# Third graph stream: weighted one-hots made on ScalarE; first experts' inner product computed transposed

## The chip, the cores and the metric

The kernel runs on one core of a Trainium2 chip. The metric is the device time of one execution in microseconds (us). The core's engines run side by side: TensorE (PE, with its weight loads shown as PEld), VectorE (DVE), ScalarE (ACT), GpSimd (POOL) and SyncE (SP), and 16 DMA engines move data. An engine executes its own instructions in the order in which they are written; engines wait for each other on semaphores.

## The reference, cut to what is computed

A graph of 6250 nodes (256 features each) and 106,250 edges sorted by target node goes through two layers. Each layer adds to `x` a graph attention of the normalised `x` and a dense mixer, then a mixture of experts. Layer 1's graph attention is itself two attention passes, so there are three edge streams: the kernel's L0, L1 and L2.

```python
xn = _layernorm(x)
x = x + _L0_gnn_ref(xn, edge_index, ...) + _L0_mix_ref(xn[None], ...)[0]
x = x + _L0_ffn_ref(_layernorm(x)[None], ...)[0]
xn = _layernorm(x)
x = x + _L1_gnn_ref(xn, ..., src, dst) + _L1_mix_ref(xn[None], ...)[0]
x = x + _L1_ffn_ref(_layernorm(x)[None], ...)[0]
# the last pass of _L1_gnn_ref (one head): the third stream
z2 = h1 @ W2.T
e2 = _leaky((z2 @ a2[:OUT_DIM])[src] + (z2 @ a2[OUT_DIM:])[dst])
alpha2 = _segment_softmax(e2, dst, n)
out = jax.ops.segment_sum(alpha2[:, None] * z2[src], dst, num_segments=n)
# _L0_ffn_ref, for each expert e of the two that a token chose
h = jax.nn.gelu(tokens @ w1[e] + b1[e], approximate=False)
y = h @ w2[e] + b2[e]
out = out + combine[:, e:e + 1] * y
```

## The kernel before

**A stream.** The edges are cut into units of 128, one edge on each partition. Two units make a slot, eight slots (16 units) a group, and there are 58 groups (`NG2`), 928 units (`NU`). For each unit GpSimd issues one indirect DMA (L1004) that gathers the 128 source rows into a ring of 48 units (three groups). `row_in` semaphores say when rows have landed; SyncE waits for the last ten units of a group and then raises `rows_there` (L981), for which VectorE waits before it adds the source scores (L1037). For each unit TensorE multiplies a 128x128 "one-hot" matrix, which says to which node of the tile each edge belongs, with the gathered rows (L1228), and VectorE adds the result of a slot into the node's sums (L1118). Every engine runs one loop over the groups; in its round `k` it computes the softmax weights of group `k`, and accumulates group `g = k - 1` in four quarters `q` of four units (`quad(g, q)` on TensorE). TensorE's and ScalarE's rounds begin when VectorE has the scores: L1037, L1039, then a transpose (L1198) and its copy `turned(k)` on ScalarE (L1292).

**Who makes the one-hots.** `Sr` holds eight of them, so two quarters. In the first two streams (L0 and L1) ScalarE's `spread(g, q)` makes four: four `Abs` of 128x128 (L1275), a wait for its own writes, and one `Relu` over all four, 128x512 (L1278); VectorE multiplies the gathered rows with the weights (L1096). In the third stream (L2, `weighted`) nothing is multiplied into the rows; VectorE makes one-hots that already carry the weight, in `weigh(g, q)`: four `tensor_scalar` of 128x128 (L1091), `is_equal` and then `mult` by a column of `WT`, the weights copied there by ScalarE's `weights(k)` (L1301). ScalarE's other work in a round is the same in all streams: two `one_hot(k + 1, v)`, each an `Abs` and a `Relu` of 128x1024 in bf16 (L1286, L1288), and `weights(k)`: `Exp` (L1298), then, after TensorE's `back(k)` (L1214, L1215), the copies (L1301 or L1303, and L1304).

**The first experts (`ffn0_*`).** Tokens are sorted into 106 tiles (`NE2`) of 128, each with one expert. GpSimd gathers a tile (L1682, ring of 12). TensorE transposes it (L1697), ScalarE copies it out (L1734, `rxe`), TensorE multiplies with the expert's first weights, picked by a register offset (L1706: the tokens are the stationary operand, the weights stream through, 256 columns), VectorE adds the bias `b1e` (L1752, `rh0`), TensorE transposes the two halves again (L1723), ScalarE applies the Gelu (L1740, `rhe`), TensorE multiplies with the second weights (L1715), VectorE adds the second bias (L1759), and SyncE writes the tile out (L1482). A product of float32 shows as two PE instructions for each `matmul` call. TensorE's loop does, in its round `r`: transposes of tile `r`, first product of tile `r - 1`, second product of `r - 3`, second transposes of `r - 2`. The routing stage ahead of it (`route0_*`) begins on TensorE when `ffn0_in` says that the router's weights, both biases and a small table have been loaded (L1475 to L1478); these four loads follow each other on SyncE's queue. The stages are separated by `meet`, where all engines wait for each other, SyncE with the last writes.

## Time and profile before

| | |
|---|---|
| median of 3 runs | 5757.75 us (5744.93 to 5762.94) |
| the profiled execution | 5751.42 us, its span 5749.6 us |
| busy over the span | PE 71%, PEld 49%, DVE 60%, ACT 48%, POOL 58% |
| third stream (3.70 to 4.94 ms) | 58 groups, about 20.7 us each |
| first experts' tiles (1.94 to 2.18 ms) | 106 tiles, about 2.17 us each |

The page of the profile gives busy shares of the whole span; the stages have different limits, so the questions below are put to views of one stage: busy time by window, instructions in order of time, and what an engine waited for. In a row of the timeline, "x4" is a merged run of four instructions with its total time, and the brackets give how long the engine had been idle before it and what ended that.

### The profile page before, as it was taken

Reading aid. Unit: us, or ns where it says so; the run is one execution under the profiler, and the core shown is the slowest. Engines: PE = TensorE matmul, PEld = TensorE weight load, DVE = VectorE, ACT = ScalarE, POOL = GpSimd, SP = SyncE. Lnnn points to the kernel's source line nnn. Section 1 sums busy time; section 2 is a strip of 40 time slices with the busy share of each in tenths; the row PEclk is TensorE's granted clock in tenths of the full one; section 3 lists DMA queues with packets and bytes.
Section 4 is the critical chain, followed back from the end, with each engine's and each line's share of the span. In section 5 each row is a group of like instructions: output and inputs, shape, how many; then the busy total and the mean of one; then the engine's idle time right before and its main releaser. Section 6 shows DMA issues by size and latency. Waiting matters only on the chain.

```text
span 5749.6 us, 74760 instructions
## 1 busy us (share of the span) xinstructions
PE 4073.4 (71%) x17795; PEld 2838.0 (49%) x17795; DVE 3468.9 (60%) x10658; ACT 2754.3 (48%) x5942; POOL 3352.1 (58%) x3492
## 2 busy tenths in 40 slices
PE   4996766666663697777777776655655656797998
PEld 3564544454443584455555555434444444333665
DVE  5377766666677537778788787745555555622111
ACT  2365666666642233578888887522222222243222
POOL 0124777777755645377777777377777777112222
PEclk9998778877875798889899898877778787898999
DMA  4293555555541333244444444344444444200110
GB/s 129 79 285 87 142 139 139 139 139 140 140 117 58 116 119 120 84 130 133 133 133 133 132 132 134 97 130 129 129 129 129 129 129 129 75 30 27 37 32 27
DMA packets 347521, 660.26 MB, mean 115 GB/s; under 512 B 78867, under 2 KB 196641, under 8 KB 346697
## 3 DMA queue, kind: packets, MB, share of 16 engines
q0 software_dynamic: 156336, 433.90, 27.8%
q1 hardware_dynamic: 180992, 213.07, 12.7%
q10 hardware_dynamic: 9772, 8.50, 0.5%
q8 instruction: 164, 2.69, 0.2%
q14 instruction: 257, 2.10, 0.1%
HBM read 541.11 MB, written 115.45 MB: 114 GB/s over the span
## 4 chain that ended last, share of the span: by engine, by line
PE 24%; issue 14%; DVE 12%; POOL 11%; DMA 5%; ACT 3%; DVEq 1%; POOLq 0%; SPq 0%; ACTq 0%
POOL AR L1004 7%; PE ps L1228 6%; DMA AR<-D_z,SRCI 4%; PE ps L2604 4%; PE ps L2585 3%; PE ps L2293 3%; POOL AR L1682 2%; PE ps L2081 2%; DVE AR L1118 1%; PE ps L2305 1%; POOL D_sx L1672 1%; PE ps L1190 1%; DVE AR L1091 1%; DVE AR L1096 1%; PE ps L2070 1%
## 5 line engine op out<-in xcount | busy, mean ns | idle before, releaser
L1004 POOL DMA_INDIRECT AR<-D_z,SRCI x1856 | 1801.3, 971 | 675.3 <-issue 496.7
L1228 PE MATMUL ps<-AR 128*128 128x264 f32 (+2 forms) x5568 | 1764.4, 471 | 212.8 <-DVE AR L1091 74.1
L1228 PEld LDWEIGHTS ps<-AR 128*128 128x128 f32 x5568 | 1240.8, 234 | 524.1 <-issue 149.9
L1004 POOL DMA_INDIRECT AR<-D_h,SRCI x904 | 872.9, 966 | 277.3 <-issue 241.6
L1118 DVE TENSOR_TENSOR AR<-ps,AR 128x264 f32 (+2 forms) x1392 | 588.2, 423 | 163.6 <-DVE AR L1118 128.2
L1275 ACT ACTIVATE AR<-iota_n,NREL 128x128 f32<-128x128 f32 x1856 | 587.3, 389 | 14.2 <-PE ps L1228 10.6
L1096 DVE TENSOR_TENSOR AR<-AR,ps 128x1024 f32<-128x1024 f32 x464 | 558.3, 1203 | 0.3 <-ACT AR L1304 0.3
L1198 PE MATMUL ps<-ident,AR 128*128 128x128 f32 (+2 forms) x174 | 61.1, 351 | 658.6 <-DVE AR L1039 658.6
L1037 DVE TENSOR_TENSOR AR<-AR 128x128 f32<-128x128 f32 (+2 forms) x174 | 49.1, 282 | 786.4 <-SPq L981 784.6
L1292 ACT ACTIVATE AR<-ps 128x128 f32<-128x128 f32 (+2 forms) x174 | 46.5, 267 | 839.1 <-PE ps L1198 834.1
L1288 ACT ACTIVATE AR<-AR,ones 128x1024 bf16<-128x1024 bf16 x348 | 399.5, 1148 | 11.3
L1286 ACT ACTIVATE AR<-AR,iota_p 128x1024 bf16<-128x1024 bf16 x348 | 394.5, 1134 | 20.3 <-DMA AR<-D_rel 20.3
L1198 PEld LDWEIGHTS ps<-ident,AR 128*128 128x128 f32 (+2 forms) x174 | 21.4, 123 | 711.8 <-issue 710.1
L1278 ACT ACTIVATE AR<-AR,ones 128x512 f32<-128x512 f32 x464 | 334.8, 722 | 15.1
L1091 DVE TENSOR_SCALAR AR<-AR,NREL 128x128 f32<-128x128 f32 x928 | 262.2, 352 | 0.0
L2516 POOL DMA_INDIRECT out<-X x57 | 56.8, 997 | 333.1 <-DVE X L2552 320.1
L1190 PE MATMUL ps<-AD,AR 128*128 x2784 | 180.3, 172 | 96.8 <-issue 46.8
L1208 PE MATMUL ps<-ones,AR 1*128 1x1 f32 (+2 forms) x696 | 73.6, 206 | 213.2 <-DVE AR L1072 212.8
L1190 PEld LDWEIGHTS ps<-AD,AR 128*128 128x128 bf16 x2784 | 135.3, 99 | 177.4 <-issue 145.8
L1298 ACT ACTIVATE AR<-AR 128x128 f32<-128x128 f32 (+2 forms) x174 | 53.8, 309 | 339.3 <-DVE AR L1082 336.5
L2585 PE MATMUL ps<-AR 128*128 x912 | 200.8, 381 | 18.3 <-ACT AR L2569 18.3
...
## 6 DMA issues: line engine op xcount, KB each, us to landing
...
AR<-D_h,SRCI POOLq DMA_INDIRECT x928
D_y<-AR SPq DMA_DIRECT2D x106, 128.0 KB, 1.7
...
```

Source lines behind the costliest of these rows:

```text
L1004: e.indirect_dma_start(out=GV[:, u % 48, :], out_offset=None, in_=D_row[L.i], in_offset=bass.IndirectOffsetOnAxis(ap=SRCI[:, u:u + 1], axi ...
L1091: t = e.tensor_scalar(Sr[:, u % 8, :], minus_n[:, :], NREL[:, u:u + 1], WT[K % 2][:, u % 16:u % 16 + 1], ALU.is_equal, ALU.mult)
L1096: e.tensor_tensor(G, G, w, ALU.mult).then_inc(m_ready, 1)
L1118: e.tensor_tensor(o, banks[n % 3][:, 0:YW], o, ALU.add).then_inc(slot_added, 1)
L1190: t = e.matmul(BK_AD[:, 3 * H * u:3 * H * u + 3 * H], OHr[v][:, 128 * (u % 8):128 * (u % 8) + 128], AD3[:, at], start=True, stop=True)
L1228: t = e.matmul(banks[n % 3][:, 0:YW], Sr[:, u % 8, :], GV[:, u % 48, L.GW - YW:L.GW], start=(i == 0), stop=(i == 1))
L1275: t = e.activation(w[:, i, :], iota_n[:, :], ACT.Abs, bias=NREL[:, u:u + 1])
L1278: e.activation(w[:, :, :], w[:, :, :], ACT.Relu, bias=ones[:, 0:1], scale=-1.0).then_inc(s_ready, 1)
L1286: e.activation(OHr[v], RBr[n % 2], ACT.Abs, bias=iota_p[:, 0:1], scale=-1.0).then_inc(*ac.up())
L1288: e.activation(OHr[v], OHr[v], ACT.Relu, bias=ones[:, 0:1], scale=-1.0).then_inc(oh_ready, 1)
L2585: t = e.matmul(ps[:, 0:256], rH2[q % 2][:, m, 128 * i:128 * i + 128], Wd[:, m, bass.ds(at, 256)], start=(m == 0), stop=(m == 7))
L2604: t = e.matmul(banks[2 + n % 4][:, 0:w], W1[:, k, 128 * m:128 * m + 128], rxt3[q % 2][:, k, 0:w], start=(k == 0), stop=(k == 1))
```

## The change

In the third stream VectorE's `weigh` makes nothing any more. ScalarE's `spread` now runs in all three streams; in the third its one `Relu` is replaced by four, one for each unit, of `weight - weight * |difference|`, with the weight as bias and its negative as scale, both read as columns (`WT` and the new `WN`, which `weights(k)` writes with one more copy). `r_ready` is waited for on ScalarE now.

In the first experts the first weights become the stationary operand: VectorE copies the expert's 128x512 block into `rw1` (ring of two, two tiles ahead), and TensorE streams the transposed tokens through its four 128x128 blocks, so the product comes out transposed. The second transposes are gone, and the Gelu reads `rh0` from SBUF in place of PSUM. The bias is loaded transposed, in two DMAs of single 4-byte elements in place of one broadcast; `ffn0_in` counts to 80 in place of 64 at all its waits.

```diff
@@ -926,7 +926,7 @@
         mark_side = AR.at
-        minus_n, WT = AR.take(128), AR.ring(2, 16)
+        WT, WN = AR.ring(2, 16), AR.ring(2, 16)
         assert AR.at <= 32156
...
         class Alone:
@@ -1087,9 +1087,6 @@
                 if L.weighted:
-                    for u in range(16 * g + 4 * q, 16 * g + 4 * q + 4):
-                        t = e.tensor_scalar(Sr[:, u % 8, :], minus_n[:, :], NREL[:, u:u + 1], WT[K % 2][:, u % 16:u % 16 + 1], ALU.is_equal, ALU.mult)
-                    t.then_inc(s_ready, 1)
                     return
...
                 w = BK_W[K % 2][:, 4 * H * q:4 * H * q + 4 * H].unsqueeze(2).to_broadcast([128, 4 * H, D])
@@ -1125,8 +1122,6 @@
             e.memset(BW[0:1, 17 * H:17 * H + 1], -BIG)
-            if L.weighted:
-                e.tensor_scalar(minus_n[:, :], iota_n[:, :], -1.0, None, ALU.mult)
             e.memset(Yv, 0.0).then_inc(y_clear, 1)
...
             at = None
@@ -1275,6 +1270,14 @@
                 e.wait_ge(*ac.now())
+                if L.weighted:
+                    p = (L.k0 + g) % 2
+                    if q == 0:
+                        e.wait_ge(r_ready, L.k0 + g + 1)
+                    for i in range(4):
+                        t = e.activation(w[:, i, :], w[:, i, :], ACT.Relu, bias=WT[p][:, 4 * q + i:4 * q + i + 1], scale=WN[p][:, 4 * q + i:4 * q + i + 1])
+                    t.then_inc(s_ready, 1)
+                    return
                 e.activation(w[:, :, :], w[:, :, :], ACT.Relu, bias=ones[:, 0:1], scale=-1.0).then_inc(s_ready, 1)
...
             def one_hot(k, v):
@@ -1299,6 +1302,7 @@
                     e.activation(WT[K % 2][:, :], w[:, 0:P], ACT.Copy)
+                    e.activation(WN[K % 2][:, :], w[:, 0:P], ACT.Copy, scale=-1.0).then_inc(*ac.up())
                 else:
...
                 e.activation(RR[:, 0:H], w[:, 128:128 + H], ACT.Exp).then_inc(r_ready, 1)
@@ -1309,24 +1313,24 @@
                     turned(k)
-                if g >= 0 and not L.weighted:
+                if g >= 0:
                     spread(g, 1)
...
                 side.after_one_hot0(e, k)
-                if g >= 0 and not L.weighted:
+                if g >= 0:
                     spread(g, 2)
...
                     one_hot(k + 1, 1)
-                if g >= 0 and not L.weighted:
+                if g >= 0:
                     spread(g, 3)
...
                 side.after_weights(e, k)
-                if k < NG2 and not L.weighted:
+                if k < NG2:
                     spread(k, 0)
...
@@ -1447,7 +1451,7 @@
         RW = AR.take(2, 8)
-        b1e, b2e = AR.take(2048), AR.take(2048)
+        b1T, b2e = AR.take(2048), AR.take(2048)
         rx = AR.ring(16, 260)
...
         smr = AR.ring(3, 5, 32)
@@ -1458,6 +1462,7 @@
         zero8 = AR.take(8)
+        rw1 = AR.ring(2, 2, 256)
         rxe, rh0, rhe = AR.ring(3, 2, 128), AR.ring(3, 256), AR.ring(3, 2, 128)
...
         AR.reset(25692)
@@ -1473,10 +1478,11 @@
             e.dma_start(RW[:, :, :], A["routerT"].rearrange("(k p) n -> p k n", p=128)).then_inc(ffn0_in, 16)
-            e.dma_start(b1e[:, :], A["L0_ffn_b1"].rearrange("e n -> (e n)").partition_broadcast(128)).then_inc(ffn0_in, 16)
+            for m in range(2):
+                e.dma_start(b1T[:, :].rearrange("p (e n) -> p e n", e=8)[:, :, m], A["L0_ffn_b1"][:, 128 * m:128 * m + 128].rearrange("e p -> p e")).then_inc(ffn0_in, 16)
             e.dma_start(b2e[:, :], A["L0_ffn_b2"].rearrange("e n -> (e n)").partition_broadcast(128)).then_inc(ffn0_in, 16)
             e.dma_start(spw[0:1, :], A["pow2"][0:120].unsqueeze(0)).then_inc(ffn0_in, 16)
-            e.wait_ge(ffn0_in, 64)
+            e.wait_ge(ffn0_in, 80)
             for s in range(NE2):
...
                 e.dma_start(D_y[128 * s:128 * s + 128, :], rO0[s % 8][:, :]).then_inc(y_out[s % 8], 16)
@@ -1656,8 +1662,8 @@
         assert end_plan + 8 * 260 <= mark_side
-        x_tr, x_xT, x_hps, x_hb, x_htr, x_h, x_ps, x_taken = [
-            early_sem(n) for n in ("x_tr", "x_xT", "x_hps", "x_hb", "x_htr", "x_h", "x_ps", "x_taken")]
+        x_tr, x_xT, x_hps, x_hb, x_h, x_ps, x_taken, x_w1 = [
+            early_sem(n) for n in ("x_tr", "x_xT", "x_hps", "x_hb", "x_h", "x_ps", "x_taken", "x_w1")]
         y_out = [early_sem(f"y_out{i}") for i in range(8)]
...
@@ -1701,9 +1707,10 @@
                         e.wait_ge(x_hb, s - 1)
-                    w = walk[0].to(s, 256, KW0, 7)
-                    for k in range(2):
-                        t = e.matmul(banks[2 + s % 2][:, 0:256], rxe[s % 3][:, k, :], WA1k[:, k, bass.ds(w, 256)], start=(k == 0), stop=(k == 1))
+                    e.wait_ge(x_w1, s + 1)
+                    for m in range(2):
+                        for k in range(2):
+                            t = e.matmul(banks[2 + s % 2][:, 128 * m:128 * m + 128], rw1[s % 2][:, k, 128 * m:128 * m + 128], rxe[s % 3][:, k, :], start=(k == 0), stop=(k == 1))
                     t.then_inc(x_hps, 1)
...
                     s = r - 3
@@ -1714,14 +1721,6 @@
                     t.then_inc(x_ps, 1)
-                if 2 <= r < NE2 + 2:
-                    s = r - 2
-                    e.wait_ge(x_hb, s + 1)
-                    if s >= 2:
-                        e.wait_ge(x_h, s - 1)
-                    for k in range(2):
-                        t = e.transpose(banks[4 + s % 2][:, 128 * k:128 * k + 128], rh0[s % 3][:, 128 * k:128 * k + 128], ident[:, :])
-                    t.then_inc(x_htr, 1)
             meet(e, 7)
...
         def ffn0_scalar(e):
@@ -1734,22 +1733,34 @@
                     s = r - 2
-                    e.wait_ge(x_htr, s + 1)
+                    e.wait_ge(x_hb, s + 1)
                     if s >= 3:
                         e.wait_ge(x_ps, s - 2)
-                    e.activation(rhe[s % 3][:, :, :], banks[4 + s % 2][:, 0:256].rearrange("p (k t) -> p k t", k=2), ACT.Gelu).then_inc(x_h, 1)
+                    e.activation(rhe[s % 3][:, :, :], rh0[s % 3][:, :].rearrange("p (m t) -> p m t", m=2), ACT.Gelu).then_inc(x_h, 1)
             meet(e, 7)
-        def ffn0_vector(e, walk1, walk):
+        def ffn0_vector(e, walk1, walk2, walk):
             route0_vector(e)
             plan0_vector(e)
+
+            def picked(s):
+
+                w = walk1.to(s, 256, KW0, 7)
+                e.tensor_copy(rw1[s % 2][:, :, :], WA1k[:, :, bass.ds(w, 256)]).then_inc(x_w1, 1)
+
+            e.wait_ge(experts_in, 64 + 128)
+            picked(0)
+            picked(1)
             for r in range(NE2 + 2):
                 if r < NE2:
-                    w = walk1.to(r, 256, KW0, 7)
+                    w = walk2.to(r, 256, KW0, 7)
                     e.wait_ge(x_hps, r + 1)
                     if r >= 3:
-                        e.wait_ge(x_htr, r - 2)
-                    e.tensor_tensor(rh0[r % 3][:, :], banks[2 + r % 2][:, 0:256], b1e[:, bass.ds(w, 256)], ALU.add).then_inc(x_hb, 1)
+                        e.wait_ge(x_h, r - 2)
+                    bias = b1T[:, bass.ds(w, 2)].unsqueeze(2).to_broadcast([128, 2, 128])
+                    e.tensor_tensor(rh0[r % 3][:, :].rearrange("p (m t) -> p m t", m=2), banks[2 + r % 2][:, 0:256].rearrange("p (m t) -> p m t", m=2), bias, ALU.add).then_inc(x_hb, 1)
+                    if r + 2 < NE2:
+                        picked(r + 2)
                 if r >= 2:
...
                     w = walk.to(s, 256, KW0, 7)
@@ -2661,7 +2672,7 @@
-            ffn0_vector(e, Walk(e, "dve1"), walk)
+            ffn0_vector(e, Walk(e, "dve1"), Walk(e, "dve2"), walk)
```

ScalarE in the third stream. Before, a whole round, from the transposed scores' copy (L1292) to the next:

```order
L1292 ACTIVATE AR<-ps 16x128 [waits t_ps]
L1286 ACTIVATE AR<-AR,iota_p 128x1024 [waits ad_ps,rb_in0]
L1288 ACTIVATE AR<-AR,ones 128x1024 [waits scalar_own]
L1286 ACTIVATE AR<-AR,iota_p 128x1024 [waits ad_ps,rb_in1]
L1288 ACTIVATE AR<-AR,ones 128x1024 [waits scalar_own]
L1298 ACTIVATE AR<-AR 16x128 [waits x_ready]
L1301 ACTIVATE AR<-ps 128x16 [waits al_ps]
L1304 ACTIVATE AR<-ps 128x1
```

After, the end of a round and the start of the next, in the changed kernel's own line numbers (L1270 and L1278 are `spread`, L1305 the new copy, L1295 the copy of the transposed scores, L1289 and L1291 the bf16 one-hot):

```order
L1304 ACTIVATE AR<-ps 128x16 [waits al_ps]
L1305 ACTIVATE AR<-ps 128x16
L1308 ACTIVATE AR<-ps 128x1
L1270 ACTIVATE AR<-iota_n,NREL 128x128 [waits slot_mm]
L1270 ACTIVATE AR<-iota_n,NREL 128x128 x3
L1278 ACTIVATE AR<-AR 128x128 [waits r_ready,scalar_own]
L1278 ACTIVATE AR<-AR 128x128 x3
L1295 ACTIVATE AR<-ps 16x128 [waits t_ps]
L1270 ACTIVATE AR<-iota_n,NREL 128x128 [waits slot_mm]
L1270 ACTIVATE AR<-iota_n,NREL 128x128 x3
L1278 ACTIVATE AR<-AR 128x128 [waits scalar_own]
L1278 ACTIVATE AR<-AR 128x128 x3
```

Eight instructions in a round became 41: four quarters of four `Abs` and four `Relu`, and the copy.

TensorE in the first experts. Before, one round of its loop:

```order
L1697 MATMUL ps<-ident,AR 128x128 [waits x_xT,row_in5]
L1697 MATMUL ps<-ident,AR 128x128
L98 REGISTER_ALU [waits x_hb,x_xT]
L99 ISA
L1706 MATMUL ps<-AR 128x256
L1706 ISA
L1706 MATMUL ps<-AR 128x256
L98 REGISTER_ALU [waits x_taken,x_h]
L99 ISA
L1715 MATMUL ps<-AR 128x256
...
L1723 MATMUL ps<-ident,AR 128x128 [waits x_h,x_hb]
L1723 MATMUL ps<-ident,AR 128x128
```

After (L1703 the transposes, L1713 the first product, L1722 the second):

```order
L1703 MATMUL ps<-ident,AR 128x128 [waits x_xT,row_in5]
L1703 MATMUL ps<-ident,AR 128x128
L1713 MATMUL ps<-AR 128x128 [waits x_w1,x_hb,x_xT]
L1713 MATMUL ps<-AR 128x128 x3
L98 REGISTER_ALU [waits x_taken,x_h]
L99 ISA
L1722 MATMUL ps<-AR 128x256
L1722 ISA
L1722 MATMUL ps<-AR 128x256
```

The first product is four calls of 128 columns with a wait for `x_w1`, and nothing stands behind the second product.

VectorE in the same loop, after (L1761 the bias on the transposed product, L1749 the copy of a weight block, L1770 the second bias); before, the rows of L1749 and the register steps ahead of it were not there:

```order
L1761 ISA [waits x_h,x_hps]
L1761 TENSOR_TENSOR AR<-ps,AR 128x256
L98 REGISTER_ALU
L99 ISA
L1749 COPY AR<-AR 128x512
L98 REGISTER_ALU
L99 ISA
L1770 ISA [waits y_out5,x_ps]
L1770 TENSOR_TENSOR AR<-ps,AR 128x256
```

The copy stands between the two additions of a round.

## Rows read from the trace of the kernel before

**Rows 1.** Busy time by window: busy us (instructions) of each engine, clock, DMA.
```profile
3730.00:4960.00 1230.00, 710.97 (x3360) 504.19 (x3361) 670.89 (x2669) 301.53 (x468) 905.27 (x917) 0.77 0.46 124
1980.00:2150.00 170.00, 169.76 (x937) 144.61 (x937) 66.26 (x156) 51.33 (x157) 71.81 (x76) 1.00 0.41 121
```

**Rows 2.** Timeline, VectorE's wait for rows: first, second, last round of third stream.
```profile
3735.75 0.19 DVE L1037 TENSOR_TENSOR AR<-AR 128x16 f32<-128x16 f32 x1 [7.17 <-SPq L981]
...
3755.72 0.19 DVE L1037 TENSOR_TENSOR AR<-AR 128x16 f32<-128x16 f32 x1 [12.27 <-SPq L981]
...
4916.77 0.19 DVE L1037 TENSOR_TENSOR AR<-AR 128x16 f32<-128x16 f32 x1 [8.87 <-SPq L981]
```

**Rows 3.** Windows of the gathers alone: second stream, third before and after round one.
```profile
2407.00:3640.00 1233.00, 883.86 (x928) 0.88 0.48 130
3711.00:3756.00 45.00, 31.97 (x34) 0.56 0.49 138
3756.00:4914.00 1158.00, 885.40 (x895) 0.78 0.48 129
```

**Rows 4.** Timeline, third stream: a gather unhindered, one stretched, VectorE's one-hots.
```profile
4337.77 0.95 POOL L1004 DMA_INDIRECT AR<-D_z,SRCI  x1 [0.30 <-issue]
...
4339.02 1.40 POOL L1004 DMA_INDIRECT AR<-D_z,SRCI  x1 [0.30 <-issue]
...
4339.40 1.08 DVE L1091 TENSOR_SCALAR AR<-AR,NREL 128x128 f32<-128x128 f32 x4
```

**Rows 5.** Timeline of ScalarE, first stream, one round and the next one's start.
```profile
1004.43 0.28 ACT L1292 ACTIVATE AR<-ps 128x128 f32<-128x128 f32 x1 [4.11 <-PE ps L1198]
1004.60 1.26 ACT L1275 ACTIVATE AR<-iota_n,NREL 128x128 f32<-128x128 f32 x4
1005.90 0.72 ACT L1278 ACTIVATE AR<-AR,ones 128x512 f32<-128x512 f32 x1
1006.53 1.13 ACT L1286 ACTIVATE AR<-AR,iota_p 128x1024 bf16<-128x1024 bf16 x1
...
1017.71 0.40 ACT L1303 ACTIVATE AR<-ps 128x128 f32<-128x128 f32 x1 [1.58 <-PE ps L1215]
...
1024.73 0.28 ACT L1292 ACTIVATE AR<-ps 128x128 f32<-128x128 f32 x1 [4.77 <-PE ps L1198]
```

**Rows 6.** Timeline of ScalarE, routing: four activations with bias and scale columns.
```profile
1798.40 2.08 ACT L1531 ACTIVATE X<-X,AR 128x256 f32<-128x256 f32 x4
```

**Rows 7.** Timeline of VectorE, end of third stream: last one-hots, last addition.
```profile
4935.91 1.12 DVE L1091 TENSOR_SCALAR AR<-AR,NREL 128x128 f32<-128x128 f32 x4
...
4939.23 0.43 DVE L1118 TENSOR_TENSOR AR<-ps,AR 128x257 f32 x1 [0.44 <-PE ps L1228]
```

**Rows 8.** Timeline of PE, first experts: one tile, to the next second transposes.
```profile
2053.54 0.38 PE L1723 MATMUL ps<-ident,AR 128*128 128x128 f32 x2
2053.75 0.38 PE L1697 MATMUL ps<-ident,AR 128*128 128x128 f32 x2
2053.97 1.03 PE L1706 MATMUL ps<-AR 128*128 x4
2054.84 1.03 PE L1715 MATMUL ps<-AR 128*128 x4
2055.70 0.38 PE L1723 MATMUL ps<-ident,AR 128*128 128x128 f32 x2
```

**Rows 9.** Timeline of PE, second experts: 32 products of 128 columns.
```profile
5732.14 3.84 PE L2604 MATMUL ps<-AR 128*128 128x128 f32 x32 [0.53 <-ACT AR L2563]
```

**Rows 10.** Timeline, end of first experts' loop: PE waits for the Gelu.
```profile
2174.48 1.13 PE L1715 MATMUL ps<-AR 128*128 x4 [0.80 <-ACT AR L1740]
```

**Rows 11.** Timeline: routing starts when the loads are there; issues behind an element-wise load.
```profile
1791.15 1.94 PE L1498 MATMUL ps<-ident,AR 128*128 128x128 f32 x8 [90.52 <-DMA AR<-in_pow]
...
3637.11 4.17 SPq L2141 DMA_DIRECT2D AR<-in_L_ffn_bg  x1
```

**Rows 12.** The page's costliest groups: a long VectorE operation on 1024 columns.
```profile
L1096 DVE TENSOR_TENSOR AR<-AR,ps 128x1024 f32<-128x1024 f32 x464 | 558.3, 1203 | 0.3 <-ACT AR L1304 0.3
```

6 lines of the change are left out of this document (3 added, 3 removed).

## The prediction

> **What bounds the kernel now.** I read busy time by stage first, because the change touches two stages and their limits differ. In the third stream no engine is full, and GpSimd is the busiest, 905 of 1230 us [rows 1]. So the next view is who waits: VectorE begins a round when the group's rows are there, after an idle 8 to 12 us [rows 2], and the last round begins 1161.05 us after the second, 20.73 us for each of 56 rounds. The gathers set that. One takes 0.95 us with 0.30 us of issue before it, 1.25 us [rows 4], and sixteen of them 20.0 us; the first interval, in which VectorE has no one-hots to make yet, is 19.97 us [rows 2]. What is between 19.97 and 20.73 is inside the gathers: their mean is 885.40 / 895 = 0.989 us after round one, 883.86 / 928 = 0.952 us in the second stream, and 0.940 us before round one of the third (31.97 / 34, the edges cut) [rows 3]. Such a stretched gather took 1.40 us with VectorE's four one-hots (L1091) in its second half [rows 4]. So the stream is bound by GpSimd's issue of gathers, and VectorE's L1091 slows it although VectorE itself is idle for 8 us in each round.
>
> In the first experts PE is busy 169.8 of 170 us at full clock, the others less than half [rows 1]. A tile is 2.16 us of PE: 0.21 us second transposes, 0.22 first transposes, 0.87 first product, 0.86 second product, by the starts of the runs [rows 8].
>
> **Third stream, pace.** Removed: 16 L1091 in a round. VectorE's 4.4 us for them (four times 1.08 [rows 4]) are beside the gathers and free nothing by themselves; what goes is the stretch. By the first interval this is (20.73 - 19.97) x 56 = 43 us; by the second stream's mean, which still has the stretches that other instructions make, (0.989 - 0.952) x 16 x 56 = 33 us. VectorE's other instructions stay, some of the stretch may come back with them at other times; I take -37 us.
>
> The one-hots are made on ScalarE now, and its round must stay under GpSimd's 20.0 us. Abs: four in 1.26 us, as in the first stream [rows 5]. Relu with bias and scale columns: four of 256 columns took 2.08 us [rows 6], 0.52 each; with 128 columns less at about 0.8 ns each (512 columns 0.72 us, 1024 columns 1.13 us [rows 5]) 0.42, four in 1.68 us, in place of one of 0.72. A quarter is 2.94 us, a round 11.8 us, to which the third stream's own 301.5 / 58 = 5.2 us [rows 1], 0.2 us for the new copy and a wait for TensorE's `back` of at most 1.6 us [rows 5] are added: 18.8 us. From the other side, the first stream's round is 1024.73 - 1004.43 - 4.77 idle = 15.53 us with its waits [rows 5]; four Relu groups now start 1.68 us apart from what follows where it was 0.63 (1006.53 - 1005.90 [rows 5]), +4.2, and the copy: 19.9 us. Both are under 20.0; I take 18.8, since ScalarE comes later to its waits and finds most of them over. Cost at this: nothing, hidden by GpSimd's gathers; without that cover each microsecond more costs 57 us.
>
> Waits that move: TensorE's quarters now wait for `s_ready` from ScalarE, and behind them on TensorE stand the rest of the round and VectorE's additions. But the last quarter of group g is done before the next round, and the gather ring gives three groups, so a gather finds its place free some 15 us ahead; GpSimd won't wait. ScalarE's `one_hot` comes up to 9 us later in the round, SyncE's loads behind it too, and both are for the next group.
>
> **Third stream, end.** After the last rows nothing covers ScalarE. Before, from L1037 to the last addition's end it took 4939.66 - 4916.77 = 22.9 us [rows 2, 7]. Now: 1.1 us to `turned`; three quarters of 2.94 us with about 0.5 for TensorE's first quarter, 10.4; `weights` 1.7 with its wait; four quarters 11.8: 23.9 us. Then the last products and addition, 2.6 us from the end of L1091 (4937.03) to 4939.66 [rows 7]. That is 26.5 us: +4 us, between +2 and +6.
>
> **First experts.** Removed per tile: 0.21 us of transposes and the product of 0.87 us [rows 8]. Added: 8 PE instructions of 128 columns; 32 of them took 3.84 us with fill and drain [rows 9], 0.11 to 0.12 each, so 0.90 to 0.96 us. Gain 0.12 to 0.18 us, 105 times: 13 to 19 us; I take -18 us, since in a full queue the fill and drain are not paid. The tile is then 1.99 us, and PE stays the bound if the others fit in. VectorE: two additions of 0.43 us (as in [rows 7]) and the copy of 512 columns, at most half of 1.20 us for 1024 [rows 12] plus some start, 0.67, at least the 0.27 of one L1091 [rows 4]: 1.1 to 1.5 us. ScalarE: two activations below 0.6 us each. GpSimd: 1.25 us a gather. PE's new wait for `x_w1`: the copy is issued two tiles ahead, behind the bias of tile s - 2, and has over 1 us to spare; behind the wait on PE stands the second product. If this cover goes, 0.1 us a tile costs 11 us. At the loop's end PE waits 0.8 us for the Gelu of each of the last two tiles [rows 10], with the transposes in that chain; they are gone: -2 us (0 to -2.5).
>
> **Routing's start.** TensorE starts when the four loads are there, at 1791.15 us [rows 11]. A broadcast of 1 MB becomes two loads of 1024 elements of 4 bytes. The nearest row is an issue behind one such load: 4.17 us [rows 11], with other loads ahead of it. Bound: -1 us (less data) to +5 us; I take +2.
>
> **Sum.** -37 + 4 - 18 - 2 + 2 = -51 us. From the profiled execution's own 5751.4 us that is 5700 us; the median of the runs is 6 us above it, which would give 5707. I say 5703 us, and put the cases below on the same footing, 3 us above what they make of the profiled execution.
>
> **A rule of the skill against the change.** The L1091 rows show what the trace has of it, 0.45 us in one gather [rows 4]. The Trainium skill, page SBUF — State Buffer, section Who interferes with whom, says that VectorE copies and scalar operations can take a port pair that GpSimd shares, as an exclusive lock for the whole instruction, and that ScalarE never waits for it. The trace agrees on L1091, by the 0.989 against 0.952 us; by the same rule the new copy in the experts puts back there what the stream loses, which is rival C.
>
> The Trainium skill, page ScalarE: Activation LUTs, section Rules for kernel authors, would keep relu and multiplication on VectorE. Engine for engine the trace agrees, 1.08 against 2.94 us for four; by that rule the result is rival B.
>
> **Rivals.** A, the stretches stay: the gathers are slowed by something that comes with the round (the scans, SyncE's loads), and L1091 only stood beside it. For: scans stand just ahead of L1091. Against: scans and loads are in the second stream too, at 0.952 us. Then 0 + 4 - 18 - 2 + 2 = -14: 5740 us.
>
> B, slower: ScalarE's round becomes the stream's. Were the Relu no shorter than 0.52 us, four 2.08, and all of the first stream's waits kept, the round is 15.53 + 4 x (2.08 - 0.63) + 0.2 = 21.5 us: (21.5 - 20.73) x 57 = +44, with the other terms +30: 5784 us. It decides from a round of 20.73 + 14 / 57 = 21.0 us. Against: the 4.77 us of idle in the first stream's round and the overlap inside the x4 runs.
>
> C, the experts gain nothing: the copy stretches each gather by its own 0.67 us and some wait, 1.25 + 0.67 + 0.2 = 2.1 us, or is held up itself until TensorE waits for `x_w1`. -51 + 18 = -33: 5721 us.
>
> **How the numbers follow.** Forecast 0.79, A 0.09, B 0.05, C 0.07. Inside the forecast the best ends give -43 + 2 - 19 - 2.5 - 1 = -63, 5691 us; the poor ones, with ScalarE's round at 20.4 us, -18 + 6 - 13 + 5 = -20, 5734 us. The range 5685 to 5735 us takes in those, C and some of the runs' own spread, and leaves out A and B. About 0.3% (17 us) is what a measurement of this kernel can tell from no change. A lies within it (-14); B is slower; the forecast and C are faster: 0.86, 0.09, 0.05.
>
> **What would show it.** Right: L1037's rounds 20.0 to 20.2 us apart with the wait for rows before each; gathers' mean under 0.96 us; ScalarE idle 1 to 2 us before `turned`; PE still full in the experts at 1.97 to 2.03 us a tile; routing's first transposes near 1793 us. Wrong: `turned` without a wait and rounds above 20.2 us (B); gathers at 0.98 us (A); PE waiting for `x_w1` or rows at 2.1 us a tile (C).

## The result, and the profile after

The changed kernel takes 5697.26 us, the median of 4 runs (5695.56 to 5704.49). The kernel before, run beside it, takes 5757.3 us. The ratio is 0.9901, with a 95% interval of 0.9889 to 0.9914, or 60 us less. The profiled executions differ by 5749.6 - 5693.8 = 55.8 us of span. The prediction was 5703 us, 5685 to 5735.

First the busy shares, from the head of the page of the kernel after:

```profile
span 5693.8 us, 76126 instructions
PE 4126.4 (72%) x18007; PEld 2893.9 (51%) x18007; DVE 3291.9 (58%) x9835; ACT 3408.7 (60%) x7856; POOL 3320.4 (58%) x3492
```

ScalarE went from 48% to 60%, VectorE from 60% to 58%, and nothing is near full over the span. These shares say where the work is, not why the time fell.

VectorE's wait for rows in the third stream, kernel after, as in [rows 2]: first, second and last round.

```profile
3711.06 0.19 DVE L1037 TENSOR_TENSOR AR<-AR 128x16 f32<-128x16 f32 x1 [7.28 <-SPq L981]
3731.09 0.19 DVE L1037 TENSOR_TENSOR AR<-AR 128x16 f32<-128x16 f32 x1 [12.18 <-SPq L981]
4859.09 0.19 DVE L1037 TENSOR_TENSOR AR<-AR 128x16 f32<-128x16 f32 x1 [8.49 <-SPq L981]
```

The wait is still there, 8 to 12 us before each round, so the gathers still set the pace. The last round begins 1128.00 us after the second, where it was 1161.05 [rows 2]: 20.14 us a round in place of 20.73. The first row also tells that 24.7 us had been saved before this stream began (3735.75 against 3711.06).

The gathers alone in these rounds, kernel after (window, its length, GpSimd's busy time and count, clock, DMA share, GB/s):

```profile
3731.00:4857.00 1126.00, 852.43 (x895) 0.74 0.48 132
```

852.43 / 895 = 0.952 us, where [rows 3] give 0.989. Thirty gathers are longer than 1.0 us; before there were 107. TensorE's granted clock was lower in these rounds than before, 0.74 against 0.78 [rows 3], and they became shorter all the same, so the clock isn't what made the gain.

ScalarE in one round of the third stream, kernel after. The brackets are idle time; lines of the same kind are left out between.

```profile
4295.40 0.27 ACT L1295 ACTIVATE AR<-ps 16x128 f32<-16x128 f32 x1 [3.13 <-PE ps L1193]
4295.58 1.26 ACT L1270 ACTIVATE AR<-iota_n,NREL 128x128 f32<-128x128 f32 x4
4296.87 1.65 ACT L1278 ACTIVATE AR<-AR 128x128 f32<-128x128 f32 x4
4298.42 1.13 ACT L1289 ACTIVATE AR<-AR,iota_p 128x1024 bf16<-128x1024 bf16 x1
...
4309.38 0.18 ACT L1304 ACTIVATE AR<-ps 128x16 f32<-128x16 f32 x1 [0.53 <-PE ps L1210]
...
4310.88 1.65 ACT L1278 ACTIVATE AR<-AR 128x128 f32<-128x128 f32 x4
4315.50 0.27 ACT L1295 ACTIVATE AR<-ps 16x128 f32<-16x128 f32 x1 [2.97 <-PE ps L1193]
```

The round is 20.10 us, and ScalarE stands idle for 2.97 us at its end, waiting for the next group's scores. So its own round is 17.1 us, and it is hidden under GpSimd's 20.0.

The end of that stream, kernel after: the last weighted Relus on ScalarE, TensorE's last products and VectorE's last addition.

```profile
4879.98 1.65 ACT L1278 ACTIVATE AR<-AR 128x128 f32<-128x128 f32 x4
...
4881.68 2.00 PE L1223 MATMUL ps<-AR 128*128 128x257 f32 x8 [0.84 <-ACT AR L1278]
...
4883.82 0.43 DVE L1115 TENSOR_TENSOR AR<-ps,AR 128x257 f32 x1 [0.44 <-PE ps L1223]
```

TensorE now waits for ScalarE here (0.84 us). From L1037 of the last round to the end of the last addition it is 25.16 us, where [rows 2, 7] gave 22.89.

The first experts, kernel after: one tile on TensorE, and what VectorE and GpSimd do beside it (L1749 is the copy of the weight block, L1770 the second bias, L1688 the gather).

```profile
2051.88 0.43 DVE L1749 COPY AR<-AR 128x512 f32 x1
2052.03 0.38 PE L1703 MATMUL ps<-ident,AR 128*128 128x128 f32 x2
2052.25 1.06 PE L1713 MATMUL ps<-AR 128*128 128x128 f32 x8
2052.37 0.42 DVE L1770 TENSOR_TENSOR AR<-ps,AR 128x256 f32<-128x256 f32 x1
2052.69 0.95 POOL L1688 DMA_INDIRECT AR<-D_sx,AR  x1 [1.03 <-PE ps L1703]
2053.14 1.03 PE L1722 MATMUL ps<-AR 128*128 x4
2054.01 0.38 PE L1703 MATMUL ps<-ident,AR 128*128 128x128 f32 x2
```

A tile is 2054.01 - 2052.03 = 1.98 us, and TensorE has no gap in it. Its parts by the starts are 0.22 (transposes), 0.89 (eight pieces of the first product) and 0.87 us (second product); the second transposes of 0.21 us [rows 8] are gone, and the first product costs 0.02 us more than before. The copy takes 0.43 us and is over when this gather starts.

The loop's end, kernel after, which answers to [rows 10]:

```profile
2148.93 1.05 PE L1713 MATMUL ps<-AR 128*128 128x128 f32 x8
2149.82 1.89 PE L1722 MATMUL ps<-AR 128*128 x8
2151.87 1.13 PE L1722 MATMUL ps<-AR 128*128 x4 [0.15 <-issue]
```

The waits for the Gelu of the last two tiles, 0.80 and 0.76 us before, are gone.

The start of routing, kernel after: the last load's issue and TensorE's first transposes, which [rows 11] had at 1791.15.

```profile
1785.56 0.29 SPq L1484 DMA_DIRECT2D AR<-in_pow  x1
1789.86 1.94 PE L1504 MATMUL ps<-ident,AR 128*128 128x128 f32 x8 [89.47 <-DMA AR<-in_pow]
```

And the last load's issue in the kernel before:

```profile
1784.75 0.29 SPq L1478 DMA_DIRECT2D AR<-in_pow  x1
```

The last issue is 0.81 us later now (there are two element-wise loads of 0.55 us each in place of one of 0.47), but the work starts 4.30 us after it in place of 6.40. The loads differ in nothing but the broadcast of 1 MB that is gone and the two small ones in its place, so the broadcast took more time on the way.

### The profile page after: what moved, and what is told of

The parts are those of the page before. It is cut to its first block, busy times and chain, and to the rows that moved or that the text cites. A ratio compares the mean times of both kernels' runs of the same rounds, so it can differ in the third digit from the quotient of the medians.

```text
span 5693.8 us, 76126 instructions
## 1 busy us (share of the span) xinstructions
PE 4126.4 (72%) x18007; PEld 2893.9 (51%) x18007; DVE 3291.9 (58%) x9835; ACT 3408.7 (60%) x7856; POOL 3320.4 (58%) x3492
## 4 chain that ended last, share of the span: by engine, by line
PE 23%; issue 14%; POOL 13%; DVE 10%; ACT 6%; DMA 3%; DVEq 1%; POOLq 0%; SPq 0%; ACTq 0%
POOL AR L1004 9%; PE ps L1223 5%; PE ps L2615 4%; PE ps L2596 4%; PE ps L2304 3%; DMA AR<-D_z,SRCI 2%; PE ps L2092 2%; POOL AR L1688 2%; PE ps L2316 1%; ACT AR L1270 1%; POOL D_sx L1678 1%; ACT AR L1278 1%; DVE AR L1093 1%; PE ps L2081 1%; DVE AR L1115 1%
## 5 line engine op out<-in xcount | busy, mean ns | idle before, releaser
L1004 POOL DMA_INDIRECT AR<-D_z,SRCI x1856 | 1767.6, 952 | 675.5 <-issue 507.8
L1223 PE MATMUL ps<-AR 128*128 128x264 f32 (+2 forms) x5568 | 1850.2, 489 | 263.1 <-ACT AR L1278 123.3
L1223 PEld LDWEIGHTS ps<-AR 128*128 128x128 f32 x5568 | 1293.4, 243 | 579.1 <-issue 155.0
L1270 ACT ACTIVATE AR<-iota_n,NREL 128x128 f32<-128x128 f32 x2784 | 880.9, 389 | 14.9 <-PE ps L1223 11.8
L1037 DVE TENSOR_TENSOR AR<-AR 128x128 f32<-128x128 f32 (+2 forms) x174 | 49.1, 282 | 726.7 <-SPq L981 724.9
L1289 ACT ACTIVATE AR<-AR,iota_p 128x1024 bf16<-128x1024 bf16 x348 | 394.6, 1134 | 20.4 <-DMA AR<-D_rel 20.4
L1291 ACT ACTIVATE AR<-AR,ones 128x1024 bf16<-128x1024 bf16 x348 | 399.5, 1148 | 11.4
L1278 ACT ACTIVATE AR<-AR 128x128 f32<-128x128 f32 x928 | 382.0, 482 | 7.7
L1295 ACT ACTIVATE AR<-ps 128x128 f32<-128x128 f32 (+2 forms) x174 | 46.7, 268 | 503.4 <-PE ps L1193 503.4
L2615 PE MATMUL ps<-AR 128*128 128x512 f32 (+1 forms) x480 | 202.6, 581 | 7.2 <-ACT AR L2574 7.2
```

The lines of the kernel that those rows point to most:

```text
L1004: e.indirect_dma_start(out=GV[:, u % 48, :], out_offset=None, in_=D_row[L.i], in_offset=bass.IndirectOffsetOnAxis(ap=SRCI[:, u:u + 1], axi ...
L1223: t = e.matmul(banks[n % 3][:, 0:YW], Sr[:, u % 8, :], GV[:, u % 48, L.GW - YW:L.GW], start=(i == 0), stop=(i == 1))
L1270: t = e.activation(w[:, i, :], iota_n[:, :], ACT.Abs, bias=NREL[:, u:u + 1])
L1278: t = e.activation(w[:, i, :], w[:, i, :], ACT.Relu, bias=WT[p][:, 4 * q + i:4 * q + i + 1], scale=WN[p][:, 4 * q + i:4 * q + i + 1])
L1289: e.activation(OHr[v], RBr[n % 2], ACT.Abs, bias=iota_p[:, 0:1], scale=-1.0).then_inc(*ac.up())
L1291: e.activation(OHr[v], OHr[v], ACT.Relu, bias=ones[:, 0:1], scale=-1.0).then_inc(oh_ready, 1)
```

## Experiments

All ran beside the kernel before. They fell on two chips. On one, called the first, the kernel before takes 5761 us, like the 5757 us above (whether it is the same chip as above is not on record; times and rounds agree); four of the kernels below ran there, and each part's heading says where. On the other, the second chip, it takes 6517 us (first four kernels) and 6509 us (next four). What is different there has a part of its own at the end of this section; until then it is enough that in that chip's third stream the rounds take 23.4 to 23.9 us whichever kernel runs, so the gathers, at 20.0 us, don't bind them. How long a gather is can still be read there.

### Each part alone, and the kernel after once more (second chip)

`e1_stream_only` has the stream's part of the diff and the experts as before, `e2_experts_only` the other way round, and `a0_after_again` is the kernel after.

> The third stream changed, the first experts as before. If the two parts are independent: the third stream as in the kernel after, 20.14 us a round (kernel before 20.73) and about 2 us more after the last rows, so -33 + 2 = -31 us, 5726 us; the experts' tiles 2.17 us, routing's first transposes at 1791.15 us. Rival: the stream gains only together with the experts' part (its position in time or the loads); then rounds above 20.3 us and over 5735 us.

> The first experts changed, the third stream as before. Independent parts: tiles 1.98 us, routing starts at 1789.9 us, the second stream begins 24.8 us earlier than in the kernel before, third stream's rounds 20.73 us; 5757 - 25 = 5732 us. Together with the stream's part -56 us, what the kernel after has. Rival: as for the other part, a sum that misses 56 us by more than 5 us.

> The kernel after, unchanged, beside the others. On a chip like the first one (kernel before 5757 us): 5697 us, rounds 20.14 us. On a chip like the second one (kernel before 6517 us, TensorE standing still for up to 9.7 us with nothing shown in its queue): the parts' differences there, +14 and -34 us, add up to -20 us, 6497 us.

| kernel, second chip | ratio to before | experts' loop, us | third stream's rounds, us | its end, us |
|---|---|---|---|---|
| e1_stream_only | 1.0022 (1.0009 to 1.0035) | 231.3 | 23.47 | 28.8 |
| e2_experts_only | 0.9954 (0.9934 to 0.9975) | 205.7 | 23.38 | 23.0 |
| a0_after_again | 0.998 (0.9964 to 0.9995) | 205.6 | 23.39 | 29.9 |

The loop is from the first tile's last addition to the last tile's; it was 228.7 us before and 205.4 after on the first chip. The experts' part gives its 23 to 26 us on both chips, and alone. The stream's part doesn't: its expected -31 us became +0.22%, about +14 us. The rounds are nearly the same with and without it (23.47 and 23.38), and the end after the last rows is 6 to 7 us longer. The numbers expected for this chip in the third kernel (sum of the two parts, -20 us, 6497 us) were near: 6492.8 us, which is 16 us under the kernel before beside it, ratio 0.998. So on this chip the two parts add up within the intervals, which are about 10 us wide to either side; on the first chip neither was run alone. The stream's part gives nothing where the gathers don't set the rounds.

### VectorE's one-hots put back as extra work, in three forms (second chip)

In `e3_vector_scalar` and, the same kernel again, `e3b_vector_scalar`, VectorE's instructions stand at their old places in the kernel after, into unused columns; nobody reads them:

```diff
                 if L.weighted:
+                    for u in range(16 * g + 4 * q, 16 * g + 4 * q + 4):
+                        e.tensor_scalar(junk_s[:, u % 4, :], iota_n[:, :], NREL[:, u:u + 1], WT[K % 2][:, u % 16:u % 16 + 1], ALU.is_equal, ALU.mult)
                     return
```

`e4_vector_tensor` and `e10_vector_psum` have another instruction in the same loop:

```diff
+                        e.tensor_tensor(junk_s[:, u % 4, :], iota_n[:, :], NREL[:, u:u + 1].to_broadcast([128, 128]), ALU.is_equal)
```
```diff
+                        e.tensor_tensor(junk_s[:, u % 4, :], banks[3][:, 0:128], iota_n[:, :], ALU.is_equal)
```

> The kernel after, with VectorE's sixteen one-hot instructions of a round put back at their old places as extra work (tensor_scalar of 128x128 with two columns, the same operations and reads but into unused columns); ScalarE's one-hots are the ones used. Theory (these instructions stretch a gather that they overlap): gathers' mean back at 0.98 to 0.99 us, rounds 20.65 to 20.75 us, 30 to 34 us longer than the kernel after, about 5729 us, with the long gathers all beside these instructions. Rival A (the stretch came with something else in the round): gathers 0.953 us, rounds 20.14 us, 5697 us, since VectorE has 8.5 us of idle time in a round for them.

> As the run before it, but the sixteen extra instructions are tensor_tensor of 128x128 (the difference column as a broadcast second tensor, is_equal), about 0.27 us each as well and at the same places. Theory (the form of the instruction matters, since tensor_tensor additions beside gathers left them at 0.95 us): gathers 0.953 us, rounds 20.14 us, 5697 us. Rival (any VectorE work of this length there does it): gathers 0.98 us and more, rounds 20.7 us, 5729 us.

> The same kernel as e3_vector_scalar (VectorE's sixteen one-hot instructions of a round put back as extra work), asked again because on the second chip the rounds weren't bound by the gathers. On a chip like the first: gathers' mean 0.985 to 1.00 us (0.998 on the second chip), rounds 20.6 to 20.8 us, 26 to 40 us longer than the kernel after. Rival (a stretch is filled from slack and ends nothing): rounds 20.14 us with gathers at 0.99 us.

> The kernel after with sixteen extra tensor_tensor of 128x128 in a round on VectorE, as in e4_vector_tensor, but one of the two inputs is read from PSUM. e4 showed that tensor_tensor with both inputs in SBUF stretches the gathers as much as tensor_scalar. New theory (two reads in SBUF, or one read at double rate, are what counts): here gathers stay at 0.953 us and rounds at 20.14 us on a chip like the first, like the additions with one input in PSUM. Rival (four of any VectorE instructions back to back do it, and the additions are only too short and apart): gathers above 0.98 us, rounds 20.6 us and more.

The gathers alone in the third stream's rounds, one row each: a0_after_again, e3b_vector_scalar, e4_vector_tensor, e10_vector_psum (columns as above).

```profile
4301.00:5610.00 1309.00, 836.45 (x880) 0.72 0.42 112
```
```profile
4346.00:5656.00 1310.00, 879.75 (x880) 0.72 0.42 112
```
```profile
4355.00:5679.00 1324.00, 894.88 (x880) 0.71 0.42 111
```
```profile
4346.00:5658.00 1312.00, 837.34 (x880) 0.72 0.42 112
```

A gather takes 0.951 us without extra work, 1.000 with tensor_scalar, 1.017 with tensor_tensor reading SBUF twice, and 0.952 with tensor_tensor reading PSUM and SBUF. The cause of the stretch is VectorE's instructions, and not something that only stood beside them (rival A). The theory that the form tensor_tensor is harmless fell with e4. What e10 changed is one of the two SBUF inputs, now in PSUM, and the stretch went with it; since that input was also a column repeated over 128 places in e4 and is a full tensor in e10, this pair alone doesn't tell the place from the repetition. `c1_psum_numbers` below moves a full input of tensor_scalar to PSUM and keeps the columns, and the stretch nearly goes there too. A gather that meets four such instructions from its start shows it best, in e4:

```profile
4410.00 1.73 POOL L1005 DMA_INDIRECT AR<-D_z,SRCI  x1 [0.30 <-issue]
4410.03 0.88 DVE L1092 TENSOR_TENSOR AR<-iota_n,NREL 128x128 f32<-128x128 f32 x4
```

and with the PSUM form, in e10:

```profile
4403.01 0.86 DVE L1092 TENSOR_TENSOR AR<-ps,iota_n 128x128 f32<-128x128 f32 x4
4403.03 0.95 POOL L1005 DMA_INDIRECT AR<-D_z,SRCI  x1 [0.30 <-issue]
```

Beside such a block, begun within 0.03 us of it, the gather takes 0.78 us more in one form and nothing in the other. The Trainium skill, page SBUF — State Buffer, section Who interferes with whom, states that a VectorE instruction with two SBUF inputs contends with a GpSimd instruction that reads SBUF; the gather reads its row numbers there. The traces agree, by 1.017 against 0.952 us.

The rounds' times and the medians (6513.83, 6513.0, 6497.84 and 6497.79 us, ratios 0.9996, 0.9996, 0.9988, 0.9981) say nothing for the question of the pace, since this chip's rounds stay at 23.4 to 23.65 us in all of them; e3 and e3b are one kernel and lie 0.15 us a round apart. Of the expectations that named a round of 20.14 or 20.7 us none could be tested here.

### Do the stretches set the pace where gathers bind? (first chip)

To be sure that GpSimd binds on any chip, every fourth gather of the third stream is issued twice in `f1_more_gathers`, the second time into unused columns, so 20 in a round; `f2_more_gathers_scalar` has the tensor_scalar of e3 on top.

```diff
+                if L.weighted and u % 4 == 3:
+                    m = u // 4
+                    if m:
+                        e.wait_ge(extra_in, 16 * m)
+                    e.indirect_dma_start(out=junk_r[:, 0:L.GW], out_offset=None, in_=D_row[L.i],
+                                         in_offset=bass.IndirectOffsetOnAxis(ap=SRCI[:, u:u + 1], axis=0)).then_inc(extra_in, 16)
```

> The kernel after, with four more gathers in each round of the third stream (every fourth is issued a second time, into unused columns), so that GpSimd is the bound on the second chip too: 20 x 1.25 = 25.0 us a round against the 23.4 us of that chip. Expected: rounds 25.0 to 25.3 us, VectorE waiting for rows again, 1.6 to 1.9 us x 57 = 90 to 110 us over the kernel after on the same chip. If rounds stay at 23.4 to 24 us, something other than the gathers' issue still ends them and the pair says nothing.

> As f1_more_gathers, with VectorE's sixteen tensor_scalar of a round put back as extra work. Theory (a stretch of the gathers lengthens the round one for one where gathers bind): gathers' mean 0.98 to 1.00 us, 20 x (0.99 - 0.953) = 0.7 to 0.9 us more a round, 40 to 50 us over f1. Rival (the stretches are taken from slack and the second chip's e3 result, 23.4 us in both cases, is the rule): same rounds as f1 within 0.2 us.

They ran on the first chip. VectorE's wait for rows in f1, second and last round, and in f2:

```profile
3737.82 0.19 DVE L1044 TENSOR_TENSOR AR<-AR 128x16 f32<-128x16 f32 x1 [17.18 <-SPq L982]
5143.31 0.19 DVE L1044 TENSOR_TENSOR AR<-AR 128x16 f32<-128x16 f32 x1 [12.66 <-SPq L982]
```
```profile
3741.42 0.19 DVE L1045 TENSOR_TENSOR AR<-AR 128x16 f32<-128x16 f32 x1 [17.15 <-SPq L983]
5190.28 0.19 DVE L1045 TENSOR_TENSOR AR<-AR 128x16 f32<-128x16 f32 x1 [13.63 <-SPq L983]
```

By 56 rounds, 25.10 us in f1, as 20 x 1.25 said, and 25.87 in f2. The medians are 5990.76 and 6036.61 us: the extra work on an engine that is idle for over 12 us in each round costs 46 us, within the 40 to 50 expected. Over both kinds the gathers' means are 0.949 and 0.987 us, and 20 times the difference is 0.76 us of the 0.77 by which a round grew. The stretch passes into the time one for one where gathers bind. On the second chip, where they don't, e3b's ratio of 0.9988 can't be told from the 0.998 of the kernel after. The 90 to 110 us that f1 was expected to cost were worked out for the second chip, where it didn't run.

Which gathers are stretched, in f2 (L1006 and L1012 are gathers):

```profile
4313.25 1.46 POOL L1006 DMA_INDIRECT AR<-D_z,SRCI  x1 [0.30 <-issue]
4313.69 1.08 DVE L1099 TENSOR_SCALAR AR<-iota_n,NREL,AR 128x128 f32<-128x128 f32 x4
4315.02 0.95 POOL L1012 DMA_INDIRECT AR<-D_z,SRCI  x1 [0.30 <-issue]
...
4317.35 1.30 DVE L1099 TENSOR_SCALAR AR<-iota_n,NREL,AR 128x128 f32<-128x128 f32 x4
4317.52 1.10 POOL L1006 DMA_INDIRECT AR<-D_z,SRCI  x1 [0.30 <-issue]
```

The long gather ends at 4314.71, 0.06 us before the block of four (4314.77); the later one at 4318.62, 0.03 us before its block. In f2 all 157 gathers above 1.0 us overlap such a block, 99 of them end within 0.1 us of its end, and none of the 822 that meet no block is long. In the kernel before it was 107, 77, and none of 576. So a held gather waits for the end of the whole row of four instructions, not of one, which shows 0.33 us. Not every gather that meets a block is held: 297 met one in f2, and 157 were long. In these two traces the blocks that begin 0.4 to 0.7 us after the gather cost the most.

That is one of two places at which a gather is held, and the other one is early. On the second chip it is the more frequent, as in e3b with the same instructions:

```profile
4443.37 1.87 POOL L1005 DMA_INDIRECT AR<-D_z,SRCI  x1 [0.30 <-issue]
4443.52 1.08 DVE L1092 TENSOR_SCALAR AR<-iota_n,NREL,AR 128x128 f32<-128x128 f32 x4
```

Here the gather goes on for 0.64 us after the block's end (4444.60). Of e3b's 79 long gathers 48 end 0.60 to 0.70 us behind a block and 12 within 0.1 us of its end; in f2 it is 4 and 99. In e4, with tensor_tensor, 118 of the 155 end 0.8 us behind the block and none at its end, and a block that began 0.4 us after the gather cost nothing there. So a gather can be held early, with 0.64 us and more of its own time still to come when the block is over, or near its end with almost none. When the block begins doesn't decide by itself whether a gather is held, and what else does isn't shown: in e3b 68 gathers met a block that began 0.12 to 0.23 us after them, and 35 of them took 0.95 us, 31 more than 1.8.

### ScalarE's round made longer (second chip)

```diff
                 if L.weighted:
+                    if q in (0, 1, 2, 3):
+                        for i in range(4):
+                            e.activation(junk_s[:, i, :], iota_n[:, :], ACT.Abs, bias=NREL[:, 16 * g + 4 * q + i:16 * g + 4 * q + i + 1])
```

> The kernel after, with four more Abs of 128x128 in each quarter of the third stream on ScalarE, into unused columns: 4 x 1.26 = 5.0 us more work a round. In the kernel after ScalarE works 17.1 us of a round of 20.14 and waits 3.0. If that is its whole work, the round becomes ScalarE's, 17.1 + 5.0 = 22.1 us, 57 rounds +113 us, and about +6 us after the last rows: 5816 us, 2.1% above the kernel after; turned without a wait, VectorE's wait for rows gone or short. Rival (its waits inside the round, for TensorE and the loads, shrink as it comes later): 21.0 to 21.5 us, 5750 to 5780 us.

6531.26 us, ratio 1.0037 (1.0024 to 1.005), 38 us over the kernel after on that chip. The rounds are 23.94 us in place of 23.39, so 17.1 + 5.0 = 22.1 us of ScalarE's work still fits for the most part in a round that something else sets, and of the 38 us about 10 are in the end after the last rows (39.5 us against 29.9). The expectation was for rounds of 20 us, so where rival B begins on the first chip is left untested. What is known of it is ScalarE's idle 2.97 us there.

### The copy beside the gather, and the loads twice (first chip)

`g3_copy_last_loads` moves VectorE's copy behind the second bias and issues the pair of bias loads once more, into unused columns:

```diff
-                    if r + 2 < NE2:
-                        picked(r + 2)
...
                     e.tensor_tensor(rO0[s % 8][:, :], banks[6 + s % 2][:, 0:256], b2e[:, bass.ds(w, 256)], ALU.add).then_inc(x_taken, 1)
+                if r + 2 < NE2:
+                    picked(r + 2)
```
```diff
+            for m in range(2):
+                e.dma_start(junk_b[:, :].rearrange("p (e n) -> p e n", e=8)[:, :, m], A["L0_ffn_b1"][:, 128 * m:128 * m + 128].rearrange("e p -> p e")).then_inc(ffn0_in, 16)
```

> The kernel after with two edits in places that don't meet. (1) In the first experts VectorE's copy of the weight block stands behind the second bias, where GpSimd's gather runs; in the kernel after both run at different times of a tile. If the copy stretches gathers as rival C had it: their mean 1.1 to 1.4 us in place of 0.957; the tile stays at 1.98 us since GpSimd has 1.0 us of idle time in each. Rival: tiles above 2.0 us. (2) The pair of element-wise bias loads is issued twice, the second time into unused columns: 1.1 us more of issue (two at 0.55) and from the first load's issue to routing's first transposes 6.47 + 1.1 = 7.6 us if only the issue counts, 8.5 us and more if the 4-byte elements take the DMA engines' time.

The last load's issue and the first transposes, and in a tile the gather (L1691) and the copy (L1752):

```profile
1790.45 0.29 SPq L1486 DMA_DIRECT2D AR<-in_pow  x1
1794.84 1.51 PE L1506 MATMUL ps<-ident,AR 128*128 128x128 f32 x6 [90.80 <-DMA AR<-in_pow]
...
2057.86 0.95 POOL L1691 DMA_INDIRECT AR<-D_sx,AR  x1 [1.03 <-PE ps L1706]
2057.92 0.43 DVE L1752 COPY AR<-AR 128x512 f32 x1
```

This kernel was run once, 5702.77 us, so it is read by its trace alone. The copy is beside the gather now, and most gathers still take 0.95 us, with the tile at 1.98 us (loop 205.2 us). The expected mean of 1.1 to 1.4 us was wrong; it is 0.961 us over the 106 gathers. That doesn't make a copy harmless: where it begins about 0.13 us before the gather, as at 1959.04 and 1959.17, the gather takes 1.12 us and ends 0.82 us after the copy, as long as e4's gathers go on behind their blocks. This happens to seven gathers of 106 here and to seven in the kernel after, between 1.01 and 1.12 us, and to none of the kernel before, where the longest takes 0.98. So rival C's mechanism exists, at 0.17 us at most and in few tiles; with 1.03 us of idle time behind each gather it costs nothing. A copy in the gather's second half wasn't tried.

From the first load's issue (1786.72) to the first transposes it is 8.12 us, against 6.47 in the kernel after, between the 7.6 and the 8.5 us expected. 1.56 of the 1.65 us lie before the last issue: the first pair of loads takes 1.10 us to issue as before, the second 1.41. From the last issue to the start it is 4.39 us where it was 4.30. So a further pair of element-wise loads costs its issue and hardly anything else.

### A version of its own (first chip)

e10 pointed to another way to take the stretch away: leave the one-hots on VectorE, but let their first input be in PSUM. `c1_psum_numbers` is the changed experts with the stream as before and one line different:

```diff
-        minus_n, WT = AR.take(128), AR.ring(2, 16)
+        minus_n, WT = banks[3][:, 0:128], AR.ring(2, 16)
```

> A version of its own: the changed experts, and in the third stream VectorE's one-hots as in the kernel before, but their first input (the negated column numbers) is kept in PSUM, in a bank that this stream doesn't use; ScalarE makes none. From e10 (one input in PSUM: gathers 0.951 us): gathers' mean 0.950 to 0.955 us. On a chip like the first: rounds 20.1 us and no longer end, 5690 to 5697 us. On the second chip, where the rounds aren't the gathers': like e2_experts_only, ratio 0.993 to 0.997, 15 to 30 us under the kernel after there. Rival (tensor_scalar stretches the gathers whatever it reads): mean 0.99 us as in e2_experts_only.

5704.52 us, ratio 0.9903 (0.9886 to 0.9919), the same as the kernel after within the intervals. It missed the 5690 to 5697 us expected, in part because the kernel before takes 4 us more here, in part by its rounds and its end. A row of its one-hots and the gather that they overlap:

```profile
4316.97 1.09 POOL L1004 DMA_INDIRECT AR<-D_z,SRCI  x1 [0.30 <-issue]
4317.68 1.33 DVE L1091 TENSOR_SCALAR AR<-ps,NREL,AR 128x128 f32<-128x128 f32 x4
```

The block ends at 4319.01 and the gather at 4318.06: it doesn't wait for the block's end any more. The gathers' mean is 0.956 us with no gather above 1.16, though 89 are above 1.0, and the rounds are 20.20 us. But four one-hots take 1.33 to 1.36 us from PSUM in place of 1.08 to 1.12 at the stream's end, VectorE is on the path after the last rows, and for eight such blocks the end is 24.8 us where it was 22.9 before. "No longer end" was expected and is wrong, and the end is hardly shorter than the kernel after's 25.2. So it gives back nothing beyond what the change gave; it only gets there with ScalarE at 48% (2756.8 us busy) in place of 60%. It wasn't run on the second chip.

### What is different on the second chip

TensorE's transpose and ScalarE's copy behind it, and TensorE's `back` and ScalarE's copy behind that, in a0_after_again on the second chip, with what VectorE was released by at the same moment:

```profile
5078.12 0.41 PE L1193 MATMUL ps<-ident,AR 128*16 128x128 f32 x1
5080.12 0.27 ACT L1295 ACTIVATE AR<-ps 16x128 f32<-16x128 f32 x1 [2.32 <-remote]
...
5093.70 0.36 PE L1210 MATMUL ps<-AR 1*128 1x1 f32 x2
5101.88 0.21 DVE L1034 TENSOR_REDUCE AR<-ps 128x16 f32<-128x48 f32 x1 [9.17 <-remote]
5101.93 0.18 ACT L1304 ACTIVATE AR<-ps 128x16 f32<-128x16 f32 x1 [8.37 <-remote]
```

From the transpose's start to the copy's it is 2.00 us here, 2.32 in the median of 54 rounds, against 0.41 in the median of the kernel after's 56 rounds above. Behind `back` ScalarE goes on 8.2 us after TensorE's instruction began, in the median 5.4, against 0.28. VectorE and ScalarE, waiting for different signals of TensorE, go on within 0.05 us of each other, long after the work that they wait for. The profile names no instruction of the core for it. So on this chip what follows on TensorE's work starts late, each round has several such steps in its chain, and the chain takes 23.4 us, more than the gathers. Whether the signals are late, or TensorE's instructions themselves end later than the trace shows (their ends are modelled), it doesn't tell, and no run here was made for it.

## Why the prediction was right, step by step

| term | predicted, us | measured, us | from |
|---|---|---|---|
| third stream, pace | -37 (-33 to -43) | -33.0 | 56 x (20.73 - 20.14) |
| third stream, end | +4 (+2 to +6) | +2.3 | 25.16 - 22.89 |
| first experts, tiles | -18 (-13 to -19) | -21.0 | loop 228.70 to 205.38, without its end |
| loop end | -2 (0 to -2.5) | -2.3 | start of last first product to start of last addition 6.48 to 4.22 |
| routing's start | +2 (-1 to +5) | -1.3 | 1791.15 to 1789.86 |
| sum | -51 | -55.3 | span -55.8 |

**Pace.** The mechanism was right, and e3 to e10 and the pair f1 and f2 show it by its cause: VectorE's one-hots stretch gathers, and a stretch is time. What was mis-sized was the choice inside -33 to -43: the stretches that the second stream also has came along, 0.952 us as there, and the first interval of 19.97 us was no picture of a whole round, since it lacks VectorE's other work. The -33 that the prediction had worked out from the second stream's mean is what came. (VectorE's 4.4 us for its one-hots should read 4.3, four times 1.08; nothing hangs on it.) In the kernel after 30 gathers are still long, and 19 of them are beside the rescale and the scans of VectorE, which read SBUF twice.

**ScalarE's cover.** Predicted 18.8 us, measured 17.1. Four Relus take 1.65 us (1.68 predicted from [rows 6]), so that step held; the term that was too large is the wait for TensorE's `back`, 1.6 us taken from the first stream and 0.53 here. Another 0.4 us is the overlap of one run with the next: a quarter is 2.85 us and not 2.94. So rival B stood 3 us of ScalarE's idle time away from this kernel, not the 1 to 2 us that the prediction named.

**End.** Too large by 1.7 us. The prediction's own sum was 26.5 against a measured 25.16 us; that it rounded 26.5 - 22.9 up to +4 is 0.4 us of the miss. Of the rest, `weights` with its wait took 1.0 us and not 1.7 (4869.11 to 4870.13), seven quarters at 2.85 us in place of 2.94 make 0.6, and ScalarE lost 0.24 us to TensorE's first quarter where 0.5 was put.

**First experts.** The tile is 1.98 us where 1.99 was predicted, by 0.02 us for the eight pieces and 0.21 for the transposes. The term was -18 and the loop gave -21, outside the term's own -13 to -19: 0.19 us for each of about 104 tiles is -19.6, the rest is something that the prediction had not seen. In the kernel before four tiles, at 1999, 2051, 2104 and 2156 us, are 2.50 us long in place of 2.17, with no wait shown; in the kernel after TensorE has none, and VectorE has such a pause at times and makes it up within the next tile.

**Routing's start.** This step failed in its sign, 3.3 us off and 0.3 us outside its own bounds. It priced two loads by an issue of 4.17 us that had stood behind other loads [rows 11]. Here an element-wise load of 1024 elements takes 0.55 us to issue, 0.70 in the second pair of g3, and the time from the last issue to the start fell by 2.1 us with a broadcast gone. g3 shows that the small loads aren't what is waited for, by doubling the pair: 1.65 us, of which 1.56 lie before the last issue.

**Rivals.** A fell with e3 and e10. B didn't come in the kernel after, where ScalarE is idle for 3 us of a round; e6, on the chip where the gathers don't bind, couldn't find its threshold. C didn't come: TensorE has no gap in the tiles, and of 106 gathers the copy stretches seven, by 0.17 us at most, where C had put 0.87 on each. The errors of the terms, +4 -1.7 -3 -0.3 -3.3, add to -4.3 us, which is the distance between -51 and -55.3. That they add to so little is in part luck: without their signs they are 12.3 us. The rest of the way from 5703 to 5697 us is that the median lies 1.7 us above the profiled execution here, and not 3 or more.

What the prediction could not see from one chip's trace is that its largest term depends on which wait ends last there. On the second chip the same diff gives 0.998, all of it and more from the experts' part.
